# Attention kernel on one core: the product of input and 1/std, and its low half, are placed in the first half of the step

## The reference

```python
xn = _layernorm(xt, norm1_g, norm1_b)            # over the 48 channels
xs = jnp.roll(xs, (-SHIFT, -SHIFT), axis=(2, 3))
qkv = (xw @ qkv_w + qkv_b)...                    # windows of 7x7 tokens, 3 heads of 16
attn = jax.nn.softmax(q @ k * dh ** (-0.5) + bias, axis=-1)
out = (attn @ v) @ proj_w + proj_b
x = x + xr                                       # first residual
xn = _layernorm(xt, norm2_g, norm2_b)
h = gelu(xn @ fc1_w + fc1_b) @ fc2_w + fc2_b
return x + h
```

## Time and profile before

| | us |
|---|---|
| median of 3 runs | 2145.37 (2136.65 to 2146.94) |
| the profiled execution | 2144.79 |
| its span, first to last instruction | 2142.8 |
| outside the span | 2.0 |
| DVE busy | 1510.8 (71%) |
| ACT busy | 1558.6 (73%) |
| POOL busy | 1174.1 (55%) |
| PE busy | 1776.0 (83%) |

### The profile page before, as it was taken

One profiled execution on the slowest core, in us unless ns is written; L12 is line 12 of the kernel. 1 busy time (PEld: TensorE's weight loads), 2 busy tenths in 40 slices (PEclk: granted clock), 3 DMA queues, 4 the chain that ended last, 5 costly groups with the idle time before them and its releaser, 6 DMA issues. The chain is left out here.

```text
span 2142.8 us, 91033 instructions
## 1 busy us (share of the span) xinstructions
PE 1776.0 (83%) x38074; PEld 1038.0 (48%) x38074; DVE 1510.8 (71%) x2025; ACT 1558.6 (73%) x2884; POOL 1174.1 (55%) x1061
## 2 busy tenths in 40 slices
PE   1469889898989889898989898884799959888884
PEld 0245555555555555555555555551466622222221
DVE  1557878777787778777777878643677757767772
ACT  1458888888888888888888888873566648767770
POOL 1357777767677767777676777652255520111111
PEclk9979999999999999999999999995799967989998
DMA  2334343434434343434344353422378759988983
GB/s 21 76 92 114 88 117 85 114 96 103 103 96 110 89 119 84 115 90 108 98 102 104 96 114 87 100 50 63 85 217 217 214 121 189 225 213 209 229 206 106
DMA packets 241103, 260.66 MB, mean 122 GB/s; under 512 B 174431, under 2 KB 188148, under 8 KB 240713
## 3 DMA queue, kind: packets, MB, share of 16 engines
q1 hardware_dynamic: 225353, 215.94, 43.0%
q0 software_dynamic: 15360, 39.08, 6.3%
HBM read 159.26 MB, written 80.99 MB: 112 GB/s over the span
## 5 line engine op out<-in xcount | busy, mean ns | idle before, releaser
L439 POOL TENSOR_TENSOR shift<-const_b,qmax 113x588 bf16<-113x588 bf16 x256 | 344.6, 1347 | 53.9 <-DVE qmax L532 53.7
L464 POOL TENSOR_TENSOR xl<-x 113x784 bf16<-113x784 f32 x64 | 136.9, 2140 | 266.5 <-DVE x L554 266.5
L518 DVE TENSOR_TENSOR xh<-X,RS 113x784 f32<-113x784 f32 x64 | 228.7, 3573 | 19.2 <-DMA RS<-rs_scratch 18.4
L1505 POOL DMA_DIRECT2D out_rolled<-r_OUT x128 | 64.0, 503 | 322.3 <-DVE r_OUT L1607 319.3
L532 DVE TENSOR_REDUCE qmax<-ps_s 113x12 f32<-113x588 f32 x256 | 194.6, 760 | 61.4 <-PE ps_s L905 61.3
L758 ACT ACTIVATE G<-ps_m 128x392 f32<-128x392 f32 x384 | 184.1, 498 | 50.7 <-PE ps_m L1005 49.8
L726 ACT ACTIVATE P<-ps_t 113x588 f32<-113x588 f32 x256 | 171.9, 672 | 66.3 <-PE ps_t L955 65.5
L1340 PE MATMUL conv_ps<-xin,band_now 64*64 64x448 bf16 x2688 | 202.3, 364 | 4.1 <-DVE x_low L1242 4.1
L429 POOL TENSOR_TENSOR xhl<-xh 113x784 bf16<-113x784 f32 x64 | 203.4, 3178 | 2.5 <-DVE xh L572 2.5
L719 ACT COPY Uf<-ps_m 113x392 f32<-113x392 f32 x384 | 172.7, 485 | 32.1 <-PE ps_m L872 24.0
L524 DVE TENSOR_TENSOR Ul<-Uf 113x784 bf16<-113x784 f32 x192 | 180.6, 966 | 0.3 <-ACT Uf L719 0.2
(11 more groups left out here) (256 smaller groups left out, 5258.6 us busy)
## 6 DMA issues: line engine op xcount, KB each, us to landing
xin<-rows_scratch SPq DMA_DIRECT2D x96, 236.0 KB, 3.7
XT<-x_tokens SPq DMA_DIRECT2D x64, 294.0 KB, 4.7
X<-x_windows SPq DMA_DIRECT2D x128, 147.0 KB, 3.0
RS<-rs_scratch SPq DMA_DIRECT2D x128, 147.0 KB, 3.4
XR<-x_windows SPq DMA_DIRECT2D x128, 147.0 KB, 3.8
x_scratch<-x SPq DMA_DIRECT2D x128, 147.0 KB, 3.9
y_scratch<-y POOLq DMA_DIRECT2D x96, 196.0 KB, 2.8
r_RS<-rs_scratch SPq DMA_DIRECT2D x128, 147.0 KB, 3.9
```

The costliest lines, as they stand in the source:

```text
L439: nc.gpsimd.tensor_tensor(shift[:, j % 2], e, m, ALU.mult).then_inc(S["md"], 1)
L464: nc.gpsimd.tensor_tensor(xl1[:], x1[:, r, :], x1m[0][:, r, :], ALU.subtract).then_inc(S["x1_lo"], 1)
L518: nc.vector.tensor_tensor(xh0[:, r, :], X[:, r, :], RS[:, r, :], ALU.mult).then_inc(S["xh0"], 1)
```

## The change

On DVE `normalise0(nx2)` moves from behind `divide(s, 1)` to a place between `divide(prv, 3)` and `first_residual(prv)`. On POOL `low0(nx2)` moves from the end of the step to a place between `make_shift(s, 2)` and `x1_low(prv)`. The wait of `normalise0` on "st" becomes earlier by half a strip (it asks for the first two quads of strip n-2, which are the readers of xh0), and a wait is added for the swap of strip n-2, which reads xh0 too. On SP the loads of X and RS go ahead of the swap, and the residual load goes behind the stores of x2.

```diff
             def step(s, image):
-                swap_halves(s.at(1))
                 x_load(s.at(2))
                 rs_load(s.at(2))
-                residual_load(s)
+                swap_halves(s.at(1))
                 tokens_load(s.at(TLEAD))
                 x2_store(s.at(-3), image)
+                residual_load(s)
                 rs_store(s.at(3))
...
                 make_shift(s, 2)
+                low0(nx2)
                 x1_low(prv)
                 low1(old)
                 make_shift(s, 3)
                 centre_tokens(s.at(4))
                 make_shift(nxt, 0)
                 squares_low(prv)
-                low0(nx2)
...
-                    wait(dve, S["st"], 4 * (s.n - 1))
+                    wait(dve, S["st"], 4 * (s.n - 2) + QUADS // 2)
+                    wait(dve, swapped[r], 64 * s.turn(2))
...
                 divide(prv, 3)
+                normalise0(nx2)
                 first_residual(prv)
                 normalise1(old)
...
                 divide(s, 1)
-                normalise0(nx2)
                 query_max(nxt, 1)
```

## The result

The changed kernel takes 2413.84 us in the median of 4 runs (2395.89 to 2429.54) against 2143.34 (2136.65 to 2146.94): a ratio of 1.126, 95% interval 1.118 to 1.135. The direction was forecast, the size was not: 2190 had been named, with 2200 as the upper end, and 270 us were lost, six times the 45 that had been worked out.

A forecast was written before the change was run, and what follows sets the result against it. No engine is full; two equally tight chains through DVE, POOL and PE set the 21.00 us step. 60 steps x 0.71 us plus 2 us at the start make 44.6 us: 2190 us, 8-in-10 range 2146 to 2200.

The forecast's parts named there:

- What bounds the kernel: Two equally tight chains through DVE, POOL and PE, ending before L1005 and L955, set the 21.00 us step.
- L518 in its old place: Removing normalise0 from DVE's step end takes away 3.84 us that nobody on the chain waits for: worth 0.
- L518 in its new place: normalise0 takes 0.96 us in DVE's idle time, making x1 late by 0.02 us at most: worth 0.
- SP: Reordered DMA issues still land in time, RS about 7 us before L518 wants it: worth 0.
- low0 in its new place: On POOL, low0 then x1_low run without pause, delaying normalise1 and divide(s,0) on DVE: 0.71 us a step.
- rival B: Ports change hands between two POOL instructions; the L524 pair's first ends 0.26 us late each step: 2163 us; chance 0.16.
- D: low1 on POOL gets in ahead of the L524 pair; second chain 1.97 us late each step: 2265 us; chance 0.08.
- C: normalise1 (L572) on DVE does not wait for POOL; the step stays 21.00 us: 2147 us; chance 0.12.
- E: Faster, if one of PE's waits hangs on L518's old place: down to 2090, some 2125 us; chance 0.12.
- Steps lengthen by what the chain is late: Whatever delays either chain closing over PE by d us lengthens each step by about d, at full granted clock.
- The range: 8 in 10, taking in A's own forecast (the 0.71 us term) and two rivals: 2146 to 2200 us.
- Start: In step 0 DVE waits for RS ahead of its work: cost 1.6, taken as 2 us, between -3 and 5.

The follow-up runs named there:

- the short hold: Kernel before, with TensorE's fc1(old, 0) also held until a GpSimd memset of 360 fp32 columns behind low1 is done: 2164.68 us, ratio 1.010.
- the fill run: Changed kernel plus 14 matmuls on constants ahead of fc1(old, 0) and 7 ahead of shift_scores(s, 3), output unread: 2241.89 us, ratio 1.047.

## Why the prediction was wrong, point by point

- *What bounds the kernel.* That two chains end before `fc1(old, 0)` and before L955 was right, that both are equally tight was not: the short hold shows room in the first. The pace was set by the second, through `divide`, the `u_low` pair, `query_max` and the last shift: in the fill run L956 came 1.63 us late and `fc1(old, 0)` 0.84, and the step grew by 1.62.
- *L518 in its old place is worth 0.* Right: with only that moved, ordinary steps stayed at 21.03 us.
- *L518 in its new place, and SP.* Right: 0.97 us in idle time, a wait for RS only at the start, DMAs landing in time. SyncE's order alone even gains 4 us.
- *low0 in its new place.* The place of the cost was right and the account of it wrong, in the step where I wrote that POOL goes on without a pause through `x1_low`. At that boundary DVE came first, as rival B had it: L573 took 1.42 us, which B had named. The rule of the Trainium skill ("SBUF — State Buffer", "Who interferes with whom") held there, one instruction at a time.
- *B's own sum, 0.26 us a step,* failed one step later: it let the L525 pair run on behind its first instruction, as in the earlier trace rows. In the run `low1` got in between, and the second L525 waited through all of it: 1.61 us. The fill run confirms the size with 1.62. The term was mis-sized by a factor of 2.3 against my 0.71. D, with a chance of 0.08, was nearest: it let `low1` in ahead of the whole pair and had 1.97 us, 2265; `low1` got in ahead of the second instruction alone.
- *C and E.* C fell with L573 at 1.42 us, not 1.02. E fell with the kernel that kept `low0` in its place: DVE was rid of 2.9 us a step and no step became shorter.
- *Steps lengthen by what the chain is late.* This is the step that failed worst, and no rival doubted it. I read the granted clock of the kernel before, found 1.00, and took it as given. It depends on TensorE's waits: with 0.93 us before `fc1(old, 0)` it never fell in 50 steps of the kernel before, with 1.3 it fell 9 times in 50, with 1.8 in all 50 and with 2.1 in 47. It cost 2.97 us a step, nearly twice the delay that set it off. The Trainium skill ("TensorE: Matmul & The Clock Gate", "HAM oscillation — how this bites in real kernels") describes this for waits for DMAs: TensorE waits between its groups of matmuls, and the clock is thrown down in every period of a loop. The trace agrees as to the falls, 50 in 50 steps, but here TensorE waits 1.8 us for DVE and not for a DMA. I had not weighed it, since the profile before showed no sign of it.
- *The range.* Its upper end, 2200, stood on the ends of one term at full clock. 60 x 1.62 = 97 us of turn-taking alone gives 2242, which lay outside it already.
- *Start.* L519 ended at 113.82 and the work behind it at 119.23, as worked out (114.1 and 119.2). But the first `project` came at 128.72, for 123.51 in the kernel before: the start cost 5.2 us, just outside my -3 to 5, and not 2; no run here was made to find the rest of it. SyncE's order alone brought it to 120.32.
- *Sums that do not come out.* With a hand-over of 0.08 us the chain is 0.65 us late, not 0.57; 60 x 0.57 with the start's -3 gives 2176, not 2178; and half the steps at E's price give some 2117, not 2125. None of them moves the forecast.

Two things stay open. One is what decides a fall of the clock, besides the length of the longest wait. In the short hold TensorE waits 1.32 us in every step, and the clock falls in some of them alone. And in the kernel with `low0` in the next step it fell in 2 of 50 steps, in one of them with waits of 0.47, 0.69 and 0.34 us and none longer (that step, 21.9 us for 20.5):

```profile
537.00:558.90 21.90, 20.35 (x490) 12.74 (x489) 17.07 (x22) 17.50 (x38) 14.34 (x11) 0.92 0.40 101
```

The other is who gets the ports when both engines want them. In the earlier trace rows L518 waited through L439 and L456, one after the other; in the earlier trace rows it got in ahead of L439; in the changed kernel DVE and GpSimd alternated at four boundaries in a row, and in the kernel with `low0` in the next step a `u_low` took 4.27 us beside L412, L439 and L456, the three that L518 waits through in its old place. By the starts in the timelines, a queue served in the order of requests fits the alternation, but neither nor the undisturbed pair of the earlier trace rows, which ran through although L429 had started ahead of it. No run here tests it.

## What to carry to other kernels

When an instruction is moved, ask not only who waits for it but who reads SBUF beside it: here a GpSimd instruction that reads and a DVE instruction with two SBUF inputs held each other up (1417 ns against 1024), and the moved 1.5 us cost 1.6 us on the path although GpSimd was idle in that place. A full granted clock in the profile before is no constant: where a change lengthens TensorE's longest wait, price a fall of the clock for the rest of the step as a case of its own. And a long instruction in a timeline may be a short one that waits; taking its wait away gains nothing unless something else, which is late, is put in its place.

## What the runs showed of the hardware that was not expected

- The clock's fall comes after the wait that sets it off: TensorE stood still from about 710.1 to 711.8, and the clock fell in the stretch of 713, and stayed at 1.2 GHz for about 10 us, in which TensorE was at work but for its wait of 0.93 us.
- Matmuls whose results nobody reads, 21 a step, shorten the step by 2.97 us when they stand where TensorE waits (22.63 for 25.60).
- With the same wait of 1.32 us in every step the clock fell in some steps only, and in 2 of 50 steps of another kernel it fell with a longest wait of 0.7 and of 1.0 us.
- A three-operand DVE instruction waits for GpSimd's reads like the two-operand one (1417 against 1024 ns), and not for GpSimd's memsets.
